# Cross-attention and feed-forward in four layers on one core: five pieces of elementwise work go from VectorE to GpSimd, with a new order table

## What is computed

```
x = x + xattn0(layernorm(x), ctx, ctx)     # strict upper triangle masked
x = x + layernorm(x) @ sign(W).T
x = x + xattn1(layernorm(x), ctx, ctx)     # causal
x = x + mixture(layernorm(x))              # 16 experts, top 2, and 2 shared ones
x = x + xattn2(ctx, layernorm(x), mask)    # q, k and v each have a layernorm with scale and bias
x = x + bitlinear_ffn(layernorm(x))        # below
x = x + xattn3(layernorm(x), ctx, ctx)     # no projections: v is ctx itself
x = x + qlora_ffn(layernorm(x))            # below
```

```
def _act_quant(x):
    scale = 127.0 / clip(max(abs(x), -1), 1e-05)
    return clip(round(x * scale), -128.0, 127.0) / scale
gate = silu(act_quant(x) @ Wg); up = act_quant(x) @ Wu
out  = act_quant(gate * up) @ Wd            # ternary weights, inner width 1024

def _dequant(q, scale):
    return (q / 7.5 - 1.0) * repeat(scale, 16, axis=1)
w = _dequant(q, scale) + lora_b @ lora_a    # six such weights of 256x256, three blocks
```

## Time and profile before

| | us |
|---|---|
| median of 3 runs | 1191.2 (1190.59 to 1201.41) |
| the profiled execution: its own time | 1198.55 |
| its span in the profile | 1196.6 |
| busy: PE / PEld / DVE / ACT / POOL | 1067.9 / 796.2 / 945.9 / 826.6 / 488.3 |
| mean granted clock of TensorE | 0.972 |

### The profile page before, as it was taken

How to read it: one execution, slowest core, us unless ns; L and a number is a source line. 1 busy time by engine, 2 the same in 40 slices (tenths; PEclk the granted TensorE clock), 3 DMA queues, 4 the chain that set the end, 5 groups by cost and what they waited for, 6 DMA issues and landing times.

```text
span 1196.6 us, 26279 instructions
## 1 busy us (share of the span) xinstructions
PE 1067.9 (89%) x8350; PEld 796.2 (67%) x8406; DVE 945.9 (79%) x3207; ACT 826.6 (69%) x1560; POOL 488.3 (41%) x1027
## 2 busy tenths in 40 slices
PE   6998999999999988899999988798899999988876
PEld 4676777777887765666677765366576766656654
DVE  3898888878555788877967798999999989898732
ACT  5777666657665666365667667457889798979953
POOL 6233356653122457657601144233334433423334
PEclk9999999999999999888999998999999999999988
DMA  7885332226777245303587752222203212121000
GB/s 221 260 275 180 87 101 71 85 76 189 218 211 213 89 121 140 85 14 116 150 259 229 233 167 80 56 69 82 82 19 87 72 54 81 53 63 54 10 10 18
DMA packets 102326, 140.03 MB, mean 117 GB/s; under 512 B 12336, under 2 KB 79792, under 8 KB 102192
## 3 DMA queue, kind: packets, MB, share of 16 engines
q1 hardware_dynamic: 99120, 129.97, 37.3%
q0 software_dynamic: 3072, 8.39, 2.2%
HBM read 65.43 MB, written 22.54 MB: 74 GB/s over the span
## 4 chain that ended last, share of the span: by engine, by line
PE 48%; DVE 20%; ACT 11%; DMA 7%; issue 6%; POOL 4%; SPq 3%; another core or an unknown queue 0%; DVEq 0%; ACTq 0%; POOLq 0%
PE ps L1516 10%; PE ps L1637 5%; PE ps L1536 4%; PE ps L1554 4%; PE ps L1729 4%; PE ps L1509 3%; DVE neg_max L2200 3%; PE ps L1523 3%; DVE ps L2196 3%; ACT probs L1945 3%; PE ps L1696 2%; DMA w<-in_expert 2%; ACT q_st L1960 2%; PE ps L1736 2%; DVE bn L2077 2%
## 5 line engine op out<-in xcount | busy, mean ns | idle before, releaser
L1945 ACT ACTIVATE probs<-ps 128x384 f32<-128x384 f32 (+1 forms) x512 | 263.5, 543 | 68.0 <-PE ps L1557 32.3
L1536 PE MATMUL ps<-k_st,q_st 96*128 96x256 bf16 (+1 forms) x1024 | 178.8, 265 | 19.4 <-DVE neg_max L2196 9.7
L1554 PE MATMUL ps<-q_st,k_st 104*128 104x256 bf16 (+1 forms) x1024 | 179.2, 263 | 14.8 <-ACT q_st L1960 6.7
L2200 DVE TENSOR_REDUCE neg_max<-ps 128x2 f32<-128x512 f32 x256 | 168.0, 679 | 11.7 <-PE ps L1536 4.9
L1960 ACT ACTIVATE q_st<-ps 8x1024 bf16<-8x1024 f32 x128 | 130.1, 1016 | 42.3 <-PE ps L1619 39.4
L2517 POOL TENSOR_SCALAR var_eps<-mv 128x2 f32<-128x2 f32 (+1 forms) x115 | 29.0, 252 | 298.0 <-DVE mv L2080 286.9
L2196 DVE CUSTOM_DVE_ANT_0 ps<-ps,diag_s 128x128 f32<-128x128 f32 (+1 forms) x384 | 123.3, 357 | 24.1 <-PE ps L1536 23.4
L1536 PEld LDWEIGHTS ps<-k_st,q_st 96*128 96x128 bf16 x1024 | 88.4, 100 | 70.3 <-DVE neg_max L2196 17.5
L1554 PEld LDWEIGHTS ps<-q_st,k_st 104*128 104x128 bf16 x1024 | 90.9, 99 | 60.3 <-issue 16.3
L1637 PE MATMUL ps<-probs,v 128*32 128x256 f32 (+1 forms) x2048 | 123.0, 359 | 4.7 <-ACT probs L1945 2.8
L2542 POOL CAST parts<-qf 128x512 bf16<-128x512 f32 x64 | 39.1, 612 | 205.2 <-DVE qf L2094 101.9
(11 more groups left out here) (270 smaller groups left out, 2545.8 us busy)
## 6 DMA issues: line engine op xcount, KB each, us to landing
k_st<-parts SPq DMA_DIRECT2D x192, 128.0 KB
q_st<-parts SPq DMA_DIRECT2D x192, 128.0 KB
w<-in_expert SPq DMA_DIRECT2D x62, 384.0 KB, 3.9
x_rows<-wo SPq DMA_DIRECT2D x10, 768.0 KB, 7.1
ctx_t<-in_ctx_t SPq DMA_DIRECT2D x16, 256.0 KB, 3.0
ring<-x_rows SPq DMA_DIRECT2D x31, 128.0 KB, 3.9
y_rows<-ring SPq DMA_DIRECT2D x31, 128.0 KB, 3.8
xn_t<-x_rows SPq DMA_DIRECT2D x31, 128.0 KB, 3.4
```

The costliest lines, as they stand in the source:

```text
L1536: last = mm(t[:, c0:c0 + n], head(q_st, r, h, KROWS, j * P, P), head(k_st, r, h, KROWS, 0, n), start=j == 0 or L != 2, stop=L != 2, skip_g ...
L1554: last = mm(t[:, j * S:j * S + n], head(k_st, r, h, KALL, j * P, P), head(q_st, r, h, KALL, skip, n), start=j == 0 or L == 3, stop=L == 3, ...
L1945: nc.scalar.activation(probs[:, (hg % 2) * HPG + h4, 0:width], tile_of(key)[:, 0:width], ACT.Exp, scale=SCALE).then_inc(*tile_drained(key))
L2200: V.tensor_reduce(neg_max[:, hg, h4, :], tile_of(key).rearrange("p (j t) -> p j t", j=SJ), AX.X, ALU.max, negate=True).then_inc(*tile_drai ...
```

## The change

Five pieces move to GpSimd, the VectorE steps around them are cut in two, and the table `AT` is new in all its numbers.

- `quantise` ends at the small instructions; `quantise_round` (GpSimd) multiplies and adds `ROUND`; `quantise_clip` (VectorE) clips.
- `hidden_quant`, `hidden_round` (GpSimd), `hidden_clip` (VectorE) likewise.
- `lora_scale` (GpSimd) makes the floats and multiplies by the scales; `lora_add` keeps the addition of the product from PSUM.
- `value_scale` is on GpSimd; `v_copy` (GpSimd) replaces `v_take` for layer 3.
- `low_load` waits for the last four expert tiles' products in place of the last one, and `block_in` waits for the low-rank weights at the first use of each n in the program's order.

```diff
@@ lanes
     part.lora(n)
     yield
+    part.lora_scale(n)
+    yield
     part.lora_add(n)
...
     part.quantise(b)
     yield
+    part.quantise_round(b)
+    yield
+    part.quantise_clip(b)
+    yield
     part.quantised(b)
...
     part.hidden_quant(T)
     yield
+    part.hidden_round(T)
+    yield
+    part.hidden_clip(T)
+    yield
     part.down_turn(T)
...
-    part.v_take(3, b)
+    part.v_copy(3, b)
@@ VectorE
-                def value_scale(b):
...
                 def lora_add(n):
-                    dve.wait_ge(*load[f"low{n}"].at(0))
-                    V.tensor_scalar(w3[:, n, :, :], w3[:, n, :, :].bitcast(I32), 1.0 / 7.5, -1.0, ALU.mult, ALU.add).then_inc(
...
-                    V.tensor_tensor(w3[:, n, :, :], w3[:, n, :, :], scale3, ALU.mult).then_inc(*prep.step(("mul", n)))
-                    dve.wait_ge(*prep.at(("mul", n)))
+                    dve.wait_ge(*lora_made.at(("mul", n)))
...
+                def quantise_clip(b):
                     if b:
                         wait_filled(dve, ("xq", b - 1))
                     for a in range(SJ):
-                        T = b * SJ + a
-                        dve.wait_ge(*quant.at(("round", T)))
...
+                        dve.wait_ge(*xq_round.at((b, a)))
...
+                def hidden_clip(T):
+                    dve.wait_ge(*hid_round.at(T))
+                    if T >= SJ:
+                        wait_filled(dve, ("ht", T - SJ))
+                    V.tensor_scalar(hid_q[:, T % SJ, :], hid[T % SJ], ROUND, Q_MAX, ALU.subtract, ALU.min).then_inc(*hid_ready.step(T))
@@ GpSimd
+                def value_scale(b):
+                    pool.wait_ge(*ln_done.at(("v", b, SJ - 1)))
+                    G.tensor_tensor(toks["v"], toks["v"], spread(V_L2VS, SJ), ALU.mult).then_inc(*tok_made.step(b))
+                    before = same_side_before(2, b)
+                    pool.wait_ge(*pv_done.at((*before, HG - 1)))
+                    pool.wait_ge(*tok_made.at(b))
+                    for a in range(SJ):
+                        G.tensor_tensor(v[:, side(2, b), a, :, 0:DH], toks["v"][:, a, :].rearrange("p (h d) -> p h d", d=DH),
+                                        vec[:, V_L2VB, :].rearrange("p (h d) -> p h d", d=DH), ALU.add).then_inc(
+                            *v_ready.step((2, b, a)))
+
+                def v_copy(L, b):
+                    pool.wait_ge(*pv_done.at((*same_side_before(L, b), HG - 1)))
+                    r = side(L, b)
+                    pool.wait_ge(*ctxn_in[b % 4].at(b))
+                    for a in range(SJ):
+                        G.tensor_copy(v[:, r, a, :, 0:DH], h_of(b)[:, a, :].rearrange("p (h d) -> p h d", d=DH)).then_inc(
+                            *v_ready.step((L, b, a)))
+
+                def lora_scale(n):
+                    pool.wait_ge(*load[f"low{n}"].at(0))
+                    G.tensor_scalar(w3[:, n, :, :], w3[:, n, :, :].bitcast(I32), 1.0 / 7.5, -1.0, ALU.mult, ALU.add).then_inc(
+                        *lora_made.step(("deq", n)))
+                    pool.wait_ge(*lora_made.at(("deq", n)))
+                    pool.wait_ge(*lora_in.at((n, 3)))
+                    G.tensor_tensor(w3[:, n, :, :], w3[:, n, :, :], scale3, ALU.mult).then_inc(*lora_made.step(("mul", n)))
+
+                def quantise_round(b):
+                    flat = xn[:, NORMED["l2f"], :, :]
+                    pool.wait_ge(*quant.at(("dq_hid", b)))
+                    for a in range(SJ):
+                        T = b * SJ + a
+                        G.tensor_scalar(flat[:, a, :], flat[:, a, :], qscale[:, T:T + 1], ROUND, ALU.mult, ALU.add).then_inc(
+                            *xq_round.step((b, a)))
+
+                def hidden_round(T):
+                    a = T % SJ
+                    h = hid[a]
+                    pool.wait_ge(*quant.at(("dqd", T)))
+                    G.tensor_scalar(h, h, hscale[:, T:T + 1], ROUND, ALU.mult, ALU.add).then_inc(*hid_round.step(T))
@@ SyncE
-                    wait_filled(sp, ("gd", NTILE - 1))
+                    for i in range(NTILE - RING, NTILE):
+                        wait_filled(sp, ("gd", i))
```

69 lines of the change are left out of this document (23 added, 46 removed), and 1070 rows, old and new, of the table AT.

## The result

| | before | after |
|---|---|---|
| runs, first timing: median (lowest to highest), 20 each | 1196.4 us (1190.6 to 1201.4) | 1187.7 us (1185.1 to 1198.3) |
| ratio, 95% interval | | 0.9938 [0.9918, 0.9957] |
| second timing, medians of 22 and 11 | 1198.3 us | 1189.9 us |
| ratio, 95% interval | | 0.9930 [0.9903, 0.9956] |
| span of the three profiled executions | 1196.6, 1196.7, 1196.6 | 1183.9, 1178.3, 1184.5 |

The changed kernel is faster, by 0.62% and 0.70% in two timings (8.7 and 8.4 us between the medians). The forecast was 1.29%, or 15.5 us, and 1175.8 us. Of the 11.9 us between 1175.8 and 1187.7, 5.2 are the base (1191.2 was the median of three runs, of twenty it is 1196.4), 6.7 the size of the effect. The profiled executions differ by more than the timed runs: 1196.6 less 1182.2, the mean of three, is 14.4 us.

A forecast was written before the change was run, and what follows sets the result against it. No engine alone bounds the kernel, but VectorE is fullest from 720 to 1080 us. Terms -18 - 4 + 1 + 3.5 + 2 = -15.5 us (1.29%) gave 1175.8 us from 1191.2; range 1155 to 1203.

The forecast's parts named there:

- Work removed and added: 42.8 us leave VectorE and 63 us come onto GpSimd; busy times near 907 and 551 us.
- Gain of the move: -18 us from 720 to 1080 us, -4 from 480 to 720, +1 for handing over, +3.5 for the lock.
- The lock: VectorE and GpSimd block each other on a shared port pair; more GpSimd work costs VectorE 3.5 us, ends 0 and 15.
- The place: VectorE, 91.7% busy, is the fullest engine from 720 to 1080 us, so its work is worth most there: 18 us.
- 18 instead of 15: 720 to 1080 us: 15 us less once TensorE is fullest, raised to 18 for the new order and VectorE's freed queue.
- what else the new table does in the first 480 us: Effects of the new order before the third layer, beyond the start: 0, with 8 us either way.
- the start's 2 us: Weight loads and a clearing put ahead of the first key and query stacks cost 2 us, ends 0 and 7.
- The hand-over: Hidden and row rounding chains crossing to GpSimd and back: mostly covered by attention work, 1 us, ends 0 and 12.
- Rival B: TensorE and ScalarE take VectorE's place on the chain, lock and start eat the rest: -3.5 us, 1188; chance 0.24.
- Rival C: Moved steps in GpSimd's in-order queue delay layer norms and what follows: slower, +30 us or 1221 (1210 at 0.75 us a step); chance 0.14.
- ScalarE's waits for `shift` in the xn group: Sign for GpSimd's queue holding up norms: 12.0 us before, below 20 expected; 40 or more would be rival C.
- the second half is shorter: Sign: third layer's start to the last attention some 22 us shorter, TensorE at 92% and VectorE near 87%.

The follow-up runs named there:

- the same run in the middle: The changed kernel's new order with all five moved pieces back on VectorE, four value_scale steps somewhat later; 1.0104 [1.0065, 1.0144] to the kernel before.

## Why the prediction missed the size

Step by step:

- Work removed and added: right in size. VectorE 904.3 us (907 forecast), GpSimd 554.6 (551), the hidden rounding 1.145 us (1.2), the value scale 1.323 (1.273 taken), the row rounding 0.482 and the copies 0.416 and 0.395 (0.33 taken, 3.2 us too little in all). That VectorE came out so near 907 is partly luck: the move took 28.9 us off its busy time and the new order, which had no term, another 12.7.
- Gain of the move, -18 - 4 + 1 + 3.5 = -17.5 us: under the new order -19.9 measured. The size is right, the terms are not where I put them, and the agreement holds for this one path only: under the old order the same move measured +19.7. The lock: VectorE's instructions that stayed rose by 3.3 us from before to after, near the 3.5 taken, but by 8.9 with the new order held (the pair alone 6.1, where 2 were taken; under the old order the pair rose by 1.9). So the share taken from the trace fits the old order, and in the new one this term was too small. The place: I let VectorE's 92% bound all of 720 to 1080 us. Behind 860 TensorE was 91% busy too, and the gain there is small (2 us of TensorE's work against before, 3.6 against the new order on VectorE). Most came from 720 to 860.
- "The order has been made anew for this division of work" was a reason for 18 instead of 15, and right as a reason: without the new order the move loses. But it was priced on one side only, as 3 us, where the difference between the two orders for this move is 3.3% (1.65 + 1.66), some 40 us.
- **The step that failed: "what else the new table does in the first 480 us has no row to price it: 0, with 8 us either way", and no term at all behind 480 us.** The new order alone costs 1.04%, 12.4 us: by the stretches of its one profile +3.2 up to (1,7), +7.5 to (2,5), +3.5 to (3,5), -4.4 to the end, of which only the second is clear of the spread of profiles. -19.9 and 12.4 make -7.5, which is what the runs show (-7.4 by the ratio); they must, since both come from the same run in the middle. With that term in place of the start's 2 us the forecast would have been -17.5 + 12.4 = -5.1 us. Only the first few microseconds of it, the start, had a price: 2 forecast, 2.5 to 5.5 measured at the first exponential in three profiles. The first 480 us, put at 0 within 8, cost some 6 us.
- The hand-over, 1 us: not contradicted for this order (VectorE waits 2.4 us in front of the clips); 26.6 us in the old.
- Rival B foresaw the size (1188 us) and not the reason: the move's gain is not hidden. Rival C's mechanism is there in the old order (norms held back by 40 us more), and the loss is near its price (+19.7 us measured, 19 to 30 worked out), though a part of that loss goes with the roundings' length and not with the norms. The changed order keeps clear of it: the move adds 3 us to the norms' waits there. The sign that I had named does not show this. ScalarE's waits for `shift` in the xn group are 14.0 us in the first profile, against 12.0 and under my bound of 20, but 18.7 in the second, 18.6 in the new order with nothing moved, and only 17.7 in the old order with the move, where rival C holds:

```profile
L1917 ACT ACTIVATE xn<-x,shift,rstd 128x256 f32<-128x256 f32 x112 | 64.1, 632 | 16.5 <-POOL shift L2515 14.0 <-DMA x_rows<-xn,dest 2.2
```

- What I had named as signs: the second half is shorter (-20.7 us from (1,7) to (3,7) in the first profile, -23.2 in the mean of three, where some 22 were forecast), with TensorE at 90.4% there by the window 720 to 1080 (325.5 of 360, where 92 was said) and VectorE at 88.8%.

What stays open: why the new order is dearer between (1,7) and (3,5) when VectorE keeps its work. It may be what an order made for a lighter VectorE does to a heavier one, and then the two numbers -19.9 and +12.4 are not two causes but two sides of one; the runs show only that neither half does without the other. Open too is the difference between profiled and timed executions: by the profiles alone (-14.4 us) the forecast of -15.5 would have been near, by the timed runs, which decide, it was twice too large. No kernel tried beats the changed one beyond its interval.

## What to carry to other kernels

An in-order schedule and the division of work among engines are one decision. Here the same 42.8 us of work, moved off a VectorE that was 92% busy in the second half, cost 1.65% under the old order and gained 1.66% under one made for it, and the new order by itself cost 1.04%. Price a new order as a term of its own, and say so when no row can. Before calling an engine the bound of a stretch, cut the stretch until the second fullest engine stops changing its share: where VectorE's 92% stood beside TensorE's 91% the gain was 2 us in 220, where TensorE had 83% it was 4 to 7 in 140. And waits at a hand-over are easily moved without gain; look at what queues behind the work on the engine that took it over.
